# Sixteen instead of fourteen score blocks per quad get their maximum by a difference of keys, with a newly written order of TensorE's work

## The chip, the cores and the metric

The kernel runs on one core of a Trainium2 chip. A core has five engines with their own instruction queues: TensorE (PE, matrix products into PSUM), VectorE (DVE), ScalarE (ACT), GpSimd (POOL) and SyncE (SP, here only the issuer of DMAs). Each engine works through its queue in order and waits on semaphores. The metric is the device time of one execution in microseconds (us); lower is better. Times of an unchanged kernel vary a little: the three runs shown lie between 1987.35 and 1992.8 us.

## The reference

The input x is 4 batches of 2048 tokens with 256 features. After a layer norm, the result is x + attention(xn) + feed-forward(xn). The feed-forward part has ternary weights, an exact GELU and a second layer norm. The attention has 16 heads of 16 dimensions, with rotary embedding on 8 of them, and is causal:

```
scores = jnp.einsum('bhqd,bhkd->bhqk', q, k) * scale
causal = jnp.tril(jnp.ones((t, t), dtype=bool))
scores = jnp.where(causal[None, None], scores, -jnp.inf)
att = jax.nn.softmax(scores, axis=-1)
y = jnp.einsum('bhqk,bhkd->bhqd', att, v)
y = y.transpose(0, 2, 1, 3).reshape(b, t, c)
return y @ Wc
```

All arithmetic is float32 in the reference. The weights are large enough that the softmax needs each row's maximum subtracted.

## The kernel before, in words

The kernel has three stages. The weights are prepared, then a loop over 16 chunks of 512 tokens computes projections and the feed-forward part, and then comes attention, which is the only stage that the change touches. Attention works on 16 *quads*: four heads of one batch. For one quad, two streams run side by side.

**The stream for maxima** finds each query row's maximum before the exponentials may be taken. For every tile `t` of 128 queries, every head and every block `k` of 512 keys up to the causal limit, TensorE writes a block of scores, queries on the partitions, into one of three PSUM buffers `sm` (L1344), and VectorE reduces it to one number per row, `pm`. There are three kinds. A *plain* block is reduced by L1277. An *edge* block is cut by the causal limit, so it is 128 to 512 keys wide, and is reduced together with a mask (L1262). A *paired* block stands for two blocks of 512 keys, k = 0 and k = 1. Since max(a, b) = a + relu(b - a), TensorE computes b - a for two heads at once from a difference of keys `DK` (L1353) into a score buffer `st`, ScalarE takes its Relu into one of three buffers `excess` (L1194), and VectorE adds that to the block k = 0 in the same instruction that takes the maximum (L1273). So a pair of paired blocks costs one ScalarE instruction of 128 x 1024 and spares VectorE two plain blocks. L1262 and L1273 leave their number in an accumulator, which a second short instruction reads.

**The stream for outputs** computes scores again with keys on the partitions and the row's maximum folded in through two extra rows, in units of two heads: TensorE writes into one of two buffers `st` (L1365), ScalarE takes the exponential into one of eight buffers `prob` (L1201), GpSimd masks the diagonal ones (L1158), and TensorE multiplies by V for four heads (L1378, sums in `pv`), which ScalarE copies out at the end of each 512 queries (L1184). The differences share the two `st` buffers with the scores.

The stream for maxima runs ahead of the stream for outputs by `AHEAD` entries: while a quad's outputs are computed, its remaining entries and the first `AHEAD` entries of the next quad are done. Entries are the blocks and seven others: three transposes of the maxima (L1340, `("rows", n)`) and four output projections of an earlier quad (L1324), which `PROJECT_AT` places. `LEAD` says how many entries before its use a difference is issued in the prologue.

TensorE's order for one quad is a string, `TIMETABLE` (L804). Each letter is one step: `m` is the next entry for maxima, `x` the next difference, `s` one unit of scores (two heads; 80 per quad), `w` one weighted sum (four heads; 40 per quad, three steps behind the scores). ScalarE follows the same string, taking only its own steps; VectorE takes the entries in their order.

```
if c == "m":
    plan.append(("entry", e // NE, e % NE))
elif c == "x":
    plan.append(("excess", x // NX, x % NX))
elif c == "s":
    plan.append(("scores", 0, u))
else:
    plan.append(("sums", -1 if n < 0 else 0, n % PAIRS))
```

TensorE waits before a difference or a unit of scores until ScalarE has read the unit that was in that `st` buffer (`exp_done`), and before an entry until VectorE has read the `sm` buffer (`sm_read`). The last quad runs the same string without the next quad's steps, and with the last output projections at places counted from `AHEAD`.

Of the kernel before, what the change touches and what calls it, by code (L numbers as in the profile page):

```python
# [744 lines left out]
GROUP_OF = {c: n for n, cs in enumerate(GROUPS) for c in cs}  # L745
LATE = 4
LEAD = 7
PROJECT_AT = (78, 91, 107, 121)
EXCESSES = 3
ROWS_LOADED = 16 * 2 * G  # L750

# [1 line left out]
def maxima_sequence():  # L753


    sequence = []
    for n, cs in enumerate(GROUPS):
        blocks = []
        for t in range(SUB * cs[0], SUB * (cs[-1] + 1)):
            c = t // SUB  # L760
            for hp in range(G // 2):
                pair = c == 3 or c == 2 and (hp == 0 or t % 2 == 1)
                for k in range(c + 1):
                    if pair and k == 1:
                        continue
                    role = "edge" if k == c else "paired" if pair and k == 0 else "plain"
                    blocks += [(role, 2 * hp + g, t, k) for g in range(2)]
        last = blocks[-1]
        sequence += blocks[:LATE] + [("rows", (n - 1) % NG)] + blocks[LATE:-1] + [last + ("ends", n)]
    for s in reversed(range(SUB)):  # L770
        sequence.insert(PROJECT_AT[s], ("project", s))
    return sequence


SEQ = maxima_sequence()
NE = len(SEQ)
PAIRED = [e for e in range(NE) if SEQ[e][0] == "paired"]
# [9 lines left out]
WIDE = 2 * CH  # L787


AHEAD = 73  # L790
XAHEAD = sum(e < AHEAD + LEAD for e in EXCESS)
LAG = 3

# [3 lines left out]
def block_width(t, k):  # L797
# [4 lines left out]


TIMETABLE = (  # L804
    "mxsmwmsmmxmsmsmmwsmwxmsmwsmsmssmwmmxwsmmsmmsmmwmmxsmwmmsmxmmwsmmxwmm"
    "smsmmsmmswsmsmxmmswssmmmxwsmmwwsmmsmmsmmswsmmmswsmmsmwsmsmmwmmssmwsm"
    "msmmmsmwsmmmswxmmmswsmmxmswsmmsssmwmmsmsmmwwmmssmmwmsmmsmwmsmsmmwmss"
    "mmwmsmmswsmmmswmsmmsmswsmmmswmsmsmmwxmmswmmsmxmmwsmsmmwsmsmmxmmswsmm"
    "s"
)  # L810


def tokens():

    plan, e, x, u, n = [], AHEAD, XAHEAD, 0, -LAG
    for c in TIMETABLE:
# [9 lines left out]
        else:  # L826
            plan.append(("sums", -1 if n < 0 else 0, n % PAIRS))
            n += 1
    assert (e, x, u, n) == (NE + AHEAD, NX + XAHEAD, 2 * PAIRS, PAIRS - LAG)
    return plan  # L830
# [4 lines left out]

EXTRA = {LATE: NE, **{AHEAD - 2 * (2 * SUB - i) + 1: NE + 1 + i for i in range(2 * SUB)}}
LAST = [("entry", 0, EXTRA[x[2]]) if x[1] == 1 else x for x in FULL if x[1] < 1 or x[0] == "entry" and x[2] in EXTRA]
# [35 lines left out]
def attention(nc, io, w, scr):  # L873

    with ExitStack() as ctx:
# [337 lines left out]
        def _(dve):  # L1213
# [74 lines left out]
            dve.wait_ge(sm_read, SM)  # L1288
            for e in range(AHEAD):
                take(0, 0, e, False)  # L1290

            def body(quad, slot, last):
                for e in range(AHEAD, NE):
                    take(quad, slot, e, last)
                    if e == INVERT_LATE and quad:
                        invert(2 * quad - 1)
                if last:
                    split_rows(quad, slot, NE, NG - 1, NG)
                    invert(2 * quad)
                    for i in range(2 * SUB):  # L1300
                        add(quad, slot, NE + 1 + i, NCH - TC + i // SUB, i % SUB)
                    return
                for e in range(AHEAD):
                    if e == INVERT_EARLY:
                        invert(2 * quad)
                    take(quad + 1, (slot + 1) % SLOTS, e, quad + 1 == NQ - 1)
# [182 lines left out]
```

## Time and profile before

| | |
|---|---|
| median of 3 runs | 1990.69 us (1987.35 to 1992.8) |
| the profiled execution's own time | 1986.25 us |
| its span, first to last instruction | 1984.5 us |
| busy over the span: PE / DVE / ACT / POOL | 94% / 86% / 81% / 28% |
| matrix clock granted, mean | 0.971 of 2.4 GHz |

Attention begins at about 524 us of the span and is three quarters of it. The busy shares over the whole span mix it with the stages ahead of it, so for this change a window inside attention is read (650 to 1860 us, some 14 quads). Two cautions: durations of instructions that follow each other on one engine overlap, so what one more instruction costs is the distance between two starts and not the duration; and ends of matrix products are modelled, so a busy TensorE may have room.

### The profile page before, as it was taken

How to read it: one execution, taken by the hardware profiler on the slowest of the kernel's cores; microseconds unless marked ns; L12 is line 12 of the kernel's file. 1: busy time of each engine (PE TensorE's matmuls, PEld its weight loads, DVE VectorE, ACT ScalarE, POOL GpSimd, SP SyncE). 2: the span in 40 equal slices, each digit the busy share in tenths (PEclk: the TensorE clock that was granted, in tenths of full speed). 3: DMA queues.
4: the chain of work that ended last, by engine and by line, in shares of the span. 5: the costliest groups of instructions: out<-in, count | busy, mean ns of one | idle time of the engine just before them, and what ended most of it. 6: DMA issues, size and time to landing. Idle time of an engine off the chain costs nothing.

```text
span 1984.5 us, 42329 instructions
## 1 busy us (share of the span) xinstructions
PE 1863.5 (94%) x13873; PEld 697.3 (35%) x13873; DVE 1703.3 (86%) x4778; ACT 1613.8 (81%) x2110; POOL 558.1 (28%) x712
## 2 busy tenths in 40 slices
PE   6799999999689999999999999999999999999986
PEld 6455556555322222222232222223222222222223
DVE  5699999999888988989898898989899898989941
ACT  2466666676169999999999999999999999999992
POOL 0112211221413424142342414234241423424111
PEclk7899999999669999999999999999999999999998
DMA  4133332336531403032241414224141431414012
GB/s 170 36 92 100 100 90 85 94 100 137 98 68 28 66 19 65 18 61 45 53 69 37 71 33 83 45 53 69 37 74 30 83 53 45 69 37 77 18 40 76
DMA packets 161366, 130.36 MB, mean 66 GB/s; under 512 B 95360, under 2 KB 145792, under 8 KB 160808
## 3 DMA queue, kind: packets, MB, share of 16 engines
q1 hardware_dynamic: 161192, 128.21, 29.8%
q8 instruction: 88, 1.44, 0.3%
q14 instruction: 86, 0.70, 0.1%
HBM read 75.79 MB, written 42.99 MB: 60 GB/s over the span
## 4 chain that ended last, share of the span: by engine, by line
PE 45%; ACT 16%; issue 3%; DVE 3%; DMA 3%; SPq 2%; POOL 1%; ACTq 0%; DVEq 0%; POOLq 0%
PE pv L1378 19%; ACT prob L1201 13%; PE st L1365 11%; PE sm L1344 9%; ACT excess L1194 3%; PE sm L1324 3%; PE st L1353 3%; DMA scratch_i<-inverse 1%; DVE pm L1277 1%; DVE sm L1273 1%; DMA Yc<-Y 1%; PE sm L1340 1%; SPq L870 1%; DVE sm L1262 0%; DMA out<-Rt 0%
## 5 line engine op out<-in xcount | busy, mean ns | idle before, releaser
L1201 ACT ACTIVATE prob<-st 128x1024 f32<-128x1024 f32 (+3 forms) x1280 | 1078.7, 900 | 71.4 <-PE st L1365 59.1
L1378 PE MATMUL pv<-prob,V 128*32 128x512 f32 (+3 forms) x5120 | 593.9, 541 | 0.2
L1262 DVE CUSTOM_DVE_ANT_0 sm<-sm,mask 128x128 f32<-128x128 f32 (+3 forms) x1024 | 492.2, 511 | 64.2 <-PE sm L1344 51.9
L1344 PE MATMUL sm<-K,Q 48*128 48x512 f16 (+3 forms) x2112 | 524.7, 349 | 15.8 <-DVE pm L1277 4.3
L1365 PE MATMUL st<-Q,K 50*128 50x512 f16 (+3 forms) x2560 | 485.3, 353 | 28.2 <-ACT prob L1201 19.9
L1158 POOL TENSOR_SCALAR_AFFINE_SELECT prob<-prob 128x256 f32<-128x256 f32 x512 | 206.2, 409 | 944.1 <-ACT prob L1201 938.7
L1277 DVE TENSOR_REDUCE pm<-sm 128x1 f32<-128x512 f32 x640 | 416.9, 684 | 23.7 <-PE sm L1344 22.1
L1273 DVE CUSTOM_DVE_ANT_0 sm<-sm,excess 128x512 f32<-128x512 f32 x448 | 311.3, 716 | 33.0 <-PE sm L1344 25.9
L1344 PEld LDWEIGHTS sm<-K,Q 48*128 48x128 f16 x2112 | 167.5, 94 | 326.0 <-DVE pm L1277 159.0
L1365 PEld LDWEIGHTS st<-Q,K 50*128 50x128 f16 x2560 | 126.9, 93 | 427.7 <-ACT prob L1201 307.7
L1194 ACT ACTIVATE excess<-st 128x1024 f32<-128x1024 f32 x219 | 225.0, 1027 | 17.8 <-PE st L1353 11.1
L1378 PEld LDWEIGHTS pv<-prob,V 128*32 128x32 f32 x5120 | 104.1, 108 | 165.8 <-issue 113.1
L1262 DVE DVE_READ_ACCUMULATOR2_ANT pm<- 128x1 f32 x1024 | 145.4, 142 | 0.2
L639 ACT ACTIVATE g<-bank 128x512 f32<-128x512 f32 x128 | 76.7, 599 | 54.8 <-PE bank L708 54.8
L669 PE MATMUL bank<-wWP,gh 128*128 128x256 f16 x512 | 113.7, 273 | 0.0
L669 PE MATMUL bank<-wWP,gl 128*128 128x256 f16 x512 | 113.5, 272 | 0.0
L1353 PE MATMUL st<-DK,Q 48*128 48x512 f16 x448 | 94.3, 388 | 18.9 <-ACT prob L1201 14.9
L533 DVE SCALAR_TENSOR_TENSOR gl<-g,wlnw,gh 128x512 f16<-128x512 f32 x128 | 92.1, 761 | 6.7 <-ACT gh L642 6.7
L642 ACT ACTIVATE gh<-g,wlnw 128x512 f16<-128x512 f32 x128 | 93.6, 731 | 0.0
L475 POOL TENSOR_TENSOR frs<-fve,wmhalf 128x4 f32<-128x4 f32 x16 | 16.3, 1018 | 274.7 <-DVE fve L603 274.7
L1324 PE MATMUL sm<-Wc,Yc 128*128 128x256 f32 x256 | 72.6, 413 | 16.2 <-POOL Yc L1138 15.5
L644 ACT ACTIVATE g<-g 128x512 f32<-128x512 f32 x128 | 81.6, 637 | 0.0
(156 smaller groups left out, 1954.6 us busy)
## 6 DMA issues: line engine op xcount, KB each, us to landing
Q<-scratch_q SPq DMA_DIRECT2D x102, 128.0 KB, 4.4
K<-scratch_k SPq DMA_DIRECT2D x102, 128.0 KB, 7.3
x<-in_x SPq DMA_DIRECT2D x18, 512.0 KB, 4.4
scratch_v<-Vs SPq DMA_DIRECT2D x64, 128.0 KB, 2.0
scratch_r<-R SPq DMA_DIRECT2D x16, 512.0 KB, 3.2
V_raw<-scratch_v SPq DMA_DIRECT2D x16, 512.0 KB, 10.0
Rt<-scratch_r SPq DMA_DIRECT2D x16, 512.0 KB, 3.9
Yc<-Y SPq DMA_DIRECT2D x128, 64.0 KB
```

Of the source, the lines that this page charges most:

```text
L669: pe.matmul(bank[s][:, 0:C], lhsT=x[:, hc, s * P:(s + 1) * P], rhs=w["WP"][:, hc, :], start=hc + k == 0, stop=hc + k == HC)
L1158: pool.affine_select(out=x, in_=x, compare_op=ALU.is_ge, fill=0.0, base=0, pattern=[[0, 2], [1, P]], channel_multiplier=-1).then_inc(maske ...
L1194: act.activation(excess[((slot + ahead) % SLOTS * NX + k) % EXCESSES][:, :, :], st[number % ST][:, :, :], ACT.Relu)\
L1201: act.activation(prob[(slot * UNITS + k) % PT][:, :, 0:width], st[number % ST][:, :, 0:width], ACT.Exp)\
L1262: dve.tensor_tensor_reduce(x, x, mask[:, CH - width:], 1.0, -3e38, ALU.add, ALU.max, pm[:, row, t, k:k + 1]).then_inc(sm_read, 1)
L1273: dve.tensor_tensor_reduce(x, x, excess[(slot * NX + r) % EXCESSES][:, h % 2, :], 1.0, -3e38, ALU.add, ALU.max, pm[:, row, t, k:k + 1]).th ...
L1277: dve.tensor_reduce(out=pm[:, row, t, k:k + 1], in_=x, axis=AX.X, op=ALU.max).then_inc(sm_read, 1)
L1324: i = pe.matmul(dst[:, 0:C], lhsT=Yc[g // TC % 2][:, a, t:t + P], rhs=Wc[:, a, :], start=a == 0, stop=a == CC - 1)
L1344: pe.matmul(dst[:, 0:block_width(t, k)], lhsT=Q[slot][r, h // 2, t * P:(t + 1) * P], rhs=K[slot][r, h // 2, k * CH:k * CH + block_width(t, ...
L1353: i = pe.matmul(st[number % ST][:, g, :], lhsT=Q[slot][rows[g], h // 2, t * P:(t + 1) * P], rhs=DK[slot][rows[g], h // 2, :], start=True, ...
L1365: i = pe.matmul(st[number % ST][:, a, 0:width], lhsT=K[slot][r, u % 2, j * P:(j + 1) * P], rhs=Q[slot][r, u % 2, (c + 1) * CH - width:(c + ...
L1378: i = pe.matmul(pv[2 * DH * h:2 * DH * (h + 1), CH - width:CH], lhsT=V[quad % VSLOTS][:, j, h, :], rhs=prob[(slot * UNITS + 2 * n + h // 2 ...
```

## The change

In `maxima_sequence`, all blocks of the third group of 512 queries (c = 2) are now paired; before, one of four pairs of heads and tiles was plain. A quad then has 16 differences in place of 14, 32 paired blocks for 28, 32 plain ones for 40, and 135 entries for 139. `AHEAD` goes from 73 to 71; the prologue makes 7 differences for 5. `PROJECT_AT` and the whole `TIMETABLE` are new (273 letters before, 271 now); of the table two lines stand here.

```
-PROJECT_AT = (78, 91, 107, 121)
+PROJECT_AT = (74, 87, 103, 117)
...
-                pair = c == 3 or c == 2 and (hp == 0 or t % 2 == 1)
+                pair = c >= 2
...
-AHEAD = 73
+AHEAD = 71
...
-    "mxsmwmsmmxmsmsmmwsmwxmsmwsmsmssmwmmxwsmmsmmsmmwmmxsmwmmsmxmmwsmmxwmm"
...
+    "wmsmsmmsmsmmwwxsmmwsmxmmswsxmmsmwwsmxmmsmmmxmsmmsmwsmmmswmmsmwsmsmms"
...
```

VectorE, in the block for c = 2 of a middle quad, between two edge blocks of 384 keys and an addition of an output projection. L1262 and its kin are one line lower after the change. Before:

```order
L1262 ISA sm1,pm<-sm1,mask 128x384 [waits sm_ready,consts]
L1262 ISA sm2,pm<-sm2,mask 128x384 [waits sm_ready,consts]
L1277 TENSOR_REDUCE pm<-sm0 128x1 [waits sm_ready]
L1277 TENSOR_REDUCE pm<-sm1 128x1 [waits sm_ready]
L1277 TENSOR_REDUCE pm<-sm2 128x1 [waits sm_ready]
L1277 TENSOR_REDUCE pm<-sm0 128x1 [waits sm_ready]
L1262 ISA sm1,pm<-sm1,mask 128x384 [waits sm_ready,consts]
L1262 ISA sm2,pm<-sm2,mask 128x384 [waits sm_ready,consts]
L1246 TENSOR_TENSOR Rt0<-Rt0,sm0 128x256 [waits r_loaded,sm_ready]
```

The same place on VectorE after the change:

```order
L1261 ISA sm2,pm<-sm2,mask 128x384 [waits sm_ready,consts]
L1261 ISA sm0,pm<-sm0,mask 128x384 [waits sm_ready,consts]
L1272 ISA sm1,pm<-sm1,excess2 128x512 [waits sm_ready,consts,exp_done]
L1272 ISA sm2,pm<-sm2,excess2 128x512 [waits sm_ready,consts,exp_done]
L1261 ISA sm0,pm<-sm0,mask 128x384 [waits sm_ready,consts]
L1261 ISA sm1,pm<-sm1,mask 128x384 [waits sm_ready,consts]
L1245 TENSOR_TENSOR Rt0<-Rt0,sm2 128x256 [waits r_loaded,sm_ready]
```

The four plain blocks have become two paired ones, which wait for ScalarE's Relu (`exp_done`) besides TensorE.

TensorE, at the end of the string and the beginning of the next quad's. Q2,K2 belong to the quad whose outputs are computed, DK0,Q0 to the next one. Before:

```order
L1365 MATMUL st1<-Q2,K2 128x128 [waits exp_done]
L1344 MATMUL sm2<-K0,Q0 128x384 [waits sm_read]
L1344 MATMUL sm0<-K0,Q0 128x512 [waits sm_read]
L1365 MATMUL st0<-Q2,K2 128x128 [waits exp_done]
L1344 MATMUL sm1<-K0,Q0 128x512 [waits sm_read,qk_loaded1,v_placed]
L1353 MATMUL st1<-DK0,Q0 128x512 [waits exp_done,differed]
L1365 MATMUL st0<-Q0,K0 128x512 [waits exp_done,m_loaded]
L1344 MATMUL sm2<-K0,Q0 128x512 [waits sm_read]
L1378 MATMUL pv<-prob2,V1 32x384 [waits masked]
```

The same place on TensorE after the change:

```order
L1364 MATMUL st1<-Q2,K2 128x128 [waits exp_done]
L1343 MATMUL sm2<-K0,Q0 128x384 [waits sm_read]
L1364 MATMUL st0<-Q2,K2 128x128 [waits exp_done]
L1352 MATMUL st1<-DK0,Q0 128x512 [waits exp_done,differed]
L1343 MATMUL sm0<-K0,Q0 128x384 [waits sm_read]
L1352 MATMUL st0<-DK0,Q0 128x512 [waits exp_done,differed]
L1343 MATMUL sm1<-K0,Q0 128x512 [waits sm_read]
L1377 MATMUL pv<-prob2,V1 32x384 [waits masked,qk_loaded1,v_placed]
L1343 MATMUL sm2<-K0,Q0 128x512 [waits sm_read]
L1364 MATMUL st1<-Q0,K0 128x512 [waits exp_done,m_loaded]
```

Two differences now stand close together here, and the first one's own entries (into `sm1` and `sm2`) follow three and five letters of the string later; before, a difference stood at least 14 letters ahead of its entry. After the change six of the 16 stand 10 letters or fewer ahead of theirs (3, 3, 7, 7, 7 and 10).

## Rows read from the trace of the kernel before

**Rows 1.** The page's first part: span, busy us, share, instructions.

```profile
span 1984.5 us, 42329 instructions
PE 1863.5 (94%) x13873; PEld 697.3 (35%) x13873; DVE 1703.3 (86%) x4778; ACT 1613.8 (81%) x2110; POOL 558.1 (28%) x712
```

**Rows 2.** The page's 40 slices: matrix clock granted, in tenths.

```profile
PEclk7899999999669999999999999999999999999998
```

**Rows 3.** Stretches: us, busy (instructions) by engine, clock, DMA, GB/s.

```profile
650.00:1860.00 1210.00, 1165.55 (x9182) 335.97 (x9183) 1091.59 (x3337) 1139.24 (x1370) 405.32 (x558) 1.00 0.29 53
524.00:564.25 40.25, 31.99 (x85) 7.99 (x87) 37.75 (x125) 5.12 (x5) 16.96 (x10) 0.50 0.54 91
1866.00:1955.90 89.90, 83.54 (x630) 26.64 (x627) 43.95 (x124) 77.58 (x94) 15.61 (x34) 1.00 0.11 26
```

**Rows 4.** GpSimd's cast of DK, once per quad: one start, and the line's summary.

```profile
687.96 1.04 POOL L1128 CAST DK<-apart 128x1024 f16<-128x1024 f32 x1
...
L1128 POOL CAST DK<-apart x16: 1037/1037/1038, 538.6 to 1814.7; 128x1024 f16<-128x1024 f32 x16
```

**Rows 5.** Chain that ended last, 650 to 1860 us, shares by line.

```profile
by line: PE pv L1378 27.1%; ACT prob L1201 17.3%; PE st L1365 15.2%; PE sm L1344 13.2%; ACT excess L1194 4.6%; issue 4.4%; PE st L1353 3.9%; PE sm L1324 3.7%; DMA scratch_i<-inverse 2.0%; DVE pm L1277 1.5%; DVE sm L1273 1.3%; SPq L870 0.8%;
```

**Rows 6.** ACT in order of time: start, us, instructions (merged), idle before.

```profile
999.93 1.93 ACT L1201 ACTIVATE prob<-st 128x1024 f32<-128x1024 f32 x2
1001.74 1.04 ACT L1194 ACTIVATE excess<-st 128x1024 f32<-128x1024 f32 x1
...
1004.87 0.60 ACT L1184 ACTIVATE Y<-pv 128x512 f32<-128x512 f32 x1
1005.36 1.02 ACT L1194 ACTIVATE excess<-st 128x1024 f32<-128x1024 f32 x1
1006.27 1.35 ACT L1201 ACTIVATE prob<-st 128x512 f32<-128x512 f32 x3
```

**Rows 7.** DVE in order of time.

```profile
1003.82 0.73 DVE L1273 CUSTOM_DVE_ANT_0 sm<-sm,excess 128x512 f32<-128x512 f32 x1
1004.47 0.14 DVE L1273 DVE_READ_ACCUMULATOR2_ANT pm<- 128x1 f32 x1
1004.47 0.73 DVE L1262 CUSTOM_DVE_ANT_0 sm<-sm,mask 128x512 f32<-128x512 f32 x1
...
1009.55 0.70 DVE L1273 CUSTOM_DVE_ANT_0 sm<-sm,excess 128x512 f32<-128x512 f32 x1
1010.17 1.28 DVE L1277 TENSOR_REDUCE pm<-sm 128x1 f32<-128x512 f32 x2
1011.37 0.27 DVE L1228 TENSOR_SCALAR mh<-sm 16x128 f16<-16x128 f32 x1
```

**Rows 8.** ACT's groups, 650 to 1860 us: busy us, mean ns, idle before, releaser.

```profile
L1201 ACT ACTIVATE prob<-st 128x1024 f32<-128x1024 f32 (+3 forms) x1118 | 942.4, 900 | 55.2 <-PE st L1365 44.3 <-issue 0.7
L1194 ACT ACTIVATE excess<-st 128x1024 f32<-128x1024 f32 x196 | 201.3, 1027 | 15.6 <-PE st L1353 9.8 <-DVE pm L1277 0.3
```

**Rows 9.** DVE's three large groups, the same window and columns.

```profile
L1262 DVE CUSTOM_DVE_ANT_0 sm<-sm,mask 128x256 f32<-128x256 f32 (+3 forms) x894 | 430.2, 511 | 56.2 <-PE sm L1344 44.9 <-issue 0.4
L1277 DVE TENSOR_REDUCE pm<-sm 128x1 f32<-128x512 f32 x560 | 364.9, 684 | 19.5 <-PE sm L1344 18.0
L1273 DVE CUSTOM_DVE_ANT_0 sm<-sm,excess 128x512 f32<-128x512 f32 x390 | 271.0, 716 | 28.4 <-PE sm L1344 22.0 <-ACT prob L1201 1.1 <-ACT excess L1194 0.5
```

**Rows 10.** PE in order of time: a sum between scores and entries.

```profile
1297.55 1.06 PE L1378 MATMUL pv<-prob,V 128*32 128x512 f32 x8
1298.55 0.39 PE L1365 MATMUL st<-Q,K 50*128 50x512 f16 x2
1298.78 0.38 PE L1344 MATMUL sm<-K,Q 48*128 48x512 f16 x1
```

**Rows 11.** ACT at 1295 to 1303 us, beside rows 10.

```profile
1294.98 5.99 ACT L1201 ACTIVATE prob<-st 128x1024 f32<-128x1024 f32 x6
1301.39 1.94 ACT L1201 ACTIVATE prob<-st 128x1024 f32<-128x1024 f32 x2 [0.41 <-PE st L1365]
```

More of the change, by code:

```diff
@@ L804 @@
 TIMETABLE = (
-    "mxsmwmsmmxmsmsmmwsmwxmsmwsmsmssmwmmxwsmmsmmsmmwmmxsmwmmsmxmmwsmmxwmm"
[L806 to L809, printed above, removed]
+    "wmsmsmmsmsmmwwxsmmwsmxmmswsxmmsmwwsmxmmsmmmxmsmmsmwsmmmswmmsmswmsmms"
+    "mmxsmmwsmmxmswsmsmmxsmwxmmwwsmmsmmsmmswsmmmswsmmswsmmmswsmmsmmswsmmm"
+    "smmsmwsmmmswsmmmxwsmmxmswsmmsxmswmmsmsmmwwmmssmmwmmsmsmwsmmmswsmmmsw"
+    "mmsmswmmsmswsmmmswsmmswsmmmswmsmsmmwxmmswsmmmswsmmxmmswsmmsmsmsxmxm"
 )
```

## The prediction

> **What bounds the kernel now.** I read first the busy line and the clock slices. Over the span TensorE, VectorE and ScalarE are all above 80% [rows 1], and the clock is full through attention apart from its start [rows 2], so neither a single engine nor the clock explains the time. Then the window inside attention: of 1210 us TensorE's rows cover 96%, ScalarE's 94% and VectorE's 90% [rows 3]. GpSimd's cast, which comes once per quad, starts at 687.96 us in the third quad and at 1814.7 us in the sixteenth [rows 4]: 13 periods in 1126.7 us, 86.67 us per quad. The window so holds 13.96 quads.
>
> Busy shares overstate the load, since durations overlap. Two exponentials take 1.93 us together, where one takes 1.02, so a unit starts 0.91 us after the one before it; a copy of `pv` is followed after 0.49 us [rows 6]. With 56 full units, 14 differences, 4 copies and 24 narrower units (8 each of 384, 256 and 128 columns per head; I estimate 0.71, 0.49 and 0.28 us, their durations less the same overlap of 0.11) ScalarE needs 51.0 + 12.7 + 2.0 + 11.8 = 77.5 us per quad. VectorE: a plain block 0.60 us (two of them from 1010.17 to 1011.37), a paired one 0.65, as from 1003.82 to 1004.47, or 0.62 at the least, as from 1009.55 to 1010.17 [rows 7]. With the edges (64 at 0.45, an estimate from their mean of 511 ns [rows 9], less the same kind of overlap) and 3.3 us of small work, estimated, it needs about 74.4 us. So ScalarE has 9.2 us and VectorE 12.3 us per quad in which they could do more. Whom they wait for: ScalarE 54 us in the window, all but for 0.3 for TensorE [rows 8]; VectorE 85 us for TensorE, 1.6 for ScalarE [rows 9]. And TensorE waits for both through the buffers. The time is lost in the coupling of three nearly full engines in fixed order: a weighted sum holds TensorE for 1.00 us before the next scores can start [rows 10], longer than a ScalarE unit, and ScalarE runs dry after it. Beside these rows six units take 5.99 us, 0.99 apart where 0.91 is possible, and then 0.41 us pass empty [rows 11]. The chain goes 63% through TensorE, 22% through ScalarE and 3% through VectorE's two named lines [rows 5].
>
> **The change, part by part.**
>
> *Two more differences on ScalarE*, per quad: 2 x 0.91 = +1.82 us of demand, 77.5 to 79.3 [rows 6].
>
> *VectorE:* 8 plain blocks go, 4 paired come: -8 x 0.60 + 4 x 0.65 = -2.2 us, 74.4 to 72.2 [rows 7].
>
> *TensorE:* four entries fewer, two pairs of difference products more. I price these by the chain, which has only what counted: L1344 holds 13.2% of 86.67 = 11.4 us over 132 blocks, 0.087 each; L1353 3.4 us over 14, 0.24 each [rows 5]. -4 x 0.087 + 2 x 0.24 = +0.13 us. GpSimd and the DMA queues get nothing new: DK is made once per quad whatever the number of differences, and the loads are the same.
>
> *What of the 1.82 lies beside other work.* First estimate, by the chain: ScalarE's lines are 21.9% of it, 19.0 us of 77.5 us of its work, so an added us is on the path for 0.245 of itself: +0.45. VectorE: 2.8%, 2.4 us of 74.4: -0.07. TensorE +0.13. Sum +0.5 us per quad. This assumes the old order. Second estimate, by the new order: I cut each string into ten stretches of eight scores units, and add for each what ScalarE and VectorE need by the prices above. The larger of the two, summed, is 80.1 us before (the second stretch for example 10.5 to 9.6, the fifth 7.3 to 6.0, the last 6.6 to 7.6, there VectorE's) and 80.3 after (10.5 to 9.3, 7.3 to 6.3, 7.5 to 7.1). That is +0.2: in four of ten stretches VectorE had been the larger, and there the added units fill time that ScalarE could not use. I take +0.2, since it sees the new order, with +0.5 inside. The bounds are far apart: all of the added work on the path, +1.82; all of VectorE's relief, -2.2. Between them the order decides, and no row of before shows it: which units find TensorE in a sum is new at every place.
>
> *Moved work.* `PROJECT_AT` and the transposes keep their places within four letters (the first projection at letter 7 for 11, the last transpose at 138 for 140), and the products are the same: 0. The sums still stand three behind.
>
> *Prologue.* 71 entries for 73 at VectorE's pace, which is busy for 37.75 of 40.25 us there while ScalarE is for 5.12 [rows 3]: -5 x 0.60 + 3 x 0.65 = -1.05 us; two more pairs of products at half clock give part back. I take -0.6, from -1.05 to +0.5. *Last quad:* 9 differences and 80 scores units as before, two entries fewer on VectorE, which is busy for 43.95 of 89.9 us: 0 [rows 3]. Cover lost here would cost 0.6 us at most.
>
> *Sum.* 15 periods x 0.2 = +3.0, less 0.6: +2.4 us on a profiled execution of 1986.25 (span 1984.5 and 1.75 around it). The median of the runs is 4.4 us above that execution; the same step on the median gives 1993.1.
>
> **The rivals.**
>
> *B, ScalarE becomes the bound (slower).* If the gaps before ScalarE's units are set by TensorE's sums and not by VectorE, they do not shrink when ScalarE has more to do, and the differences come on top. For it: ScalarE is the fuller of the two by rows and is 22% of the chain against 3%. Against it: the gaps are 9.2 us per quad, and the new order may place the differences in them. Between half and all of 1.82 us, 1.37 x 15 = +20.5, less 0.6: 2010.6; at full price 2017. It decides from where ScalarE's 9.2 us per quad do not fall below 8.3. The Trainium skill's page "Perfetto Trace Analysis" (Identifying the Most-Contended Engine) says to find the engine with the highest occupancy among VectorE, ScalarE and GpSimd and to optimize that first; here that is ScalarE, 94% against 90%, and the change moves work onto it. By that rule this rival is what happens. The trace agrees with the occupancies, and the chain with the sign, but not with its size.
>
> *C, VectorE's relief and the order get through (faster).* For it: VectorE waited for TensorE in 85 us of the window, and each such wait, once TensorE had come late, was handed back through three `sm` buffers; 2.2 us less work lets it catch up sooner. Three entries in a row before a unit of scores ("mmms") stand 10 times in the string for 6, places at which TensorE can refill all three `sm` buffers before it goes on. A difference's buffer has been read 11 letters or more before it is wanted again, for 6 before. If 1.0 us per quad goes, between 0.5 and 2.2: -15 less 0.6: 1975. Against it: the chain hardly touches VectorE.
>
> *D, VectorE waits for ScalarE (slower).* Six differences stand close ahead of their entries. At the end of the string the difference has at most one unit in front of it on ScalarE, so its Relu ends about 2 x 0.91 + 0.2 us after the product was issued, and TensorE, which needs `exp_done` of that same unit before it can issue the next difference or scores, brings the entry 1.2 to 1.6 us after. A wait of 0.2 to 0.8 us at six places: 1.2 to 4.8 us per quad on VectorE. Behind the waiting block stand the other two `sm` buffers, and then TensorE's next entry, and the scores behind that. VectorE has 12.3 us free, so I charge a fifth to a quarter, at most 1.0 us: +15, 2005. Before, such waits were 1.6 us in the whole window.
>
> ScalarE's price per element also speaks on the choice of engine. A Relu unit of 1024 columns takes 0.91 us and spares two plain blocks of 512, 1.20 us, at 2 x 0.05 more for the paired ones. The Trainium skill's page "ScalarE: Activation LUTs" (Rules for kernel authors) says to put relu and max on VectorE and not on ScalarE. By the rule moving them is a loss; on these float32 blocks out of PSUM the trace has ScalarE the faster one per column, 0.89 ns against 1.17, so I do not follow it beyond rival B.
>
> **How the numbers follow.** This kernel's measurement tells about 0.3%, 6 us, from no change. My forecast, the loads nearly cancel, has 0.36, with an own range of -0.4 to +0.6 us per quad, 1984 to 2000; of it 0.04 are faster by more than 6 us, 0.05 slower, 0.27 the same. C has 0.34, of which 0.01 is within 6 us. B has 0.24, D 0.06, together 0.28 slower and 0.02 the same. Faster 0.37, same 0.30, slower 0.33. The range takes in C to a little beyond its middle and B to its middle: 1973 to 2011.
>
> **What would show it.** Counts per quad: 16 Relus, 32 paired and 32 plain blocks. The period by GpSimd's cast: 86.9 us if I am right, 85.7 under C, 88.0 under B. ScalarE's idle in a window of 14 quads: 71 us before [rows 8]; in my case it falls to about 50, in B it stays near 65, in C it falls to 40 or below. VectorE's waits on exponentials or Relus: under 10 us in the window if D is wrong, 17 to 67 if it is right. VectorE's share falls from 90% to about 87%, and under C its waits for TensorE fall as well. I am wrong if the period moves by more than 0.6 us either way, and wrong in kind if the difference lies in the prologue or the last quad.

## The result: 0.28% faster, and the profile after

| | before | after |
|---|---|---|
| median (14 runs each) | 1991.54 us (1985.04 to 1995.04) | 1985.78 us (1981.33 to 1988.33) |
| profiled execution, its span | 1986.25, 1984.5 us | 1983.96, 1982.0 us |

The ratio is 0.9972, 95% interval 0.9962 to 0.9982: a small gain, clear of noise, at the edge of what I had called no change, and on the other side of the forecast of 1993.

The page's first two parts for the changed kernel; they answer to [rows 1, 2].

```profile
span 1982.0 us, 42489 instructions
PE 1851.7 (93%) x13873; PEld 695.8 (35%) x13873; DVE 1669.6 (84%) x4778; ACT 1637.0 (83%) x2142; POOL 556.0 (28%) x712
...
PEclk8899999999769999999999999999999999999998
```

ScalarE has 23 us more of busy rows, VectorE 34 us less. The stretch 650 to 1860 us, for [rows 3]:

```profile
650.00:1860.00 1210.00, 1157.20 (x9196) 335.77 (x9198) 1064.00 (x3343) 1160.73 (x1400) 404.87 (x560) 1.00 0.29 53
```

ScalarE's share went from 94% to 96%, VectorE's from 90% to 88%. GpSimd's cast of DK, one start per quad, before (two more than in [rows 4]) and after:

```profile
1034.28 1.04 POOL L1128 CAST DK<-apart 128x1024 f16<-128x1024 f32 x1
1121.28 1.04 POOL L1128 CAST DK<-apart 128x1024 f16<-128x1024 f32 x1
```

```profile
1035.48 1.04 POOL L1127 CAST DK<-apart 128x1024 f16<-128x1024 f32 x1
1121.82 1.04 POOL L1127 CAST DK<-apart 128x1024 f16<-128x1024 f32 x1
...
1812.68 1.04 POOL L1127 CAST DK<-apart 128x1024 f16<-128x1024 f32 x1
```

From 1121 us on eight periods take 86.68 us each before (to 1814.7) and 86.36 after. ScalarE's groups and its idle time after, for [rows 8]:

```profile
L1200 ACT ACTIVATE prob<-st 128x1024 f32<-128x1024 f32 (+3 forms) x1120 | 942.6, 902 | 22.3 <-PE st L1364 13.1
L1193 ACT ACTIVATE excess<-st 128x1024 f32<-128x1024 f32 x224 | 229.0, 1029 | 26.2 <-PE st L1352 10.6 <-PE st L1364 5.5 <-DVE pm L1261 4.8
```

The recorded idle before them fell from 71 to 49 us in 14 quads. VectorE's, for [rows 9]:

```profile
L1261 DVE CUSTOM_DVE_ANT_0 sm<-sm,mask 128x256 f32<-128x256 f32 (+3 forms) x895 | 431.7, 511 | 74.5 <-PE sm L1343 68.0 <-issue 0.4
L1272 DVE CUSTOM_DVE_ANT_0 sm<-sm,excess 128x512 f32<-128x512 f32 x448 | 307.0, 718 | 50.5 <-PE sm L1343 40.4 <-ACT prob L1200 7.0
L1276 DVE TENSOR_REDUCE pm<-sm 128x1 f32<-128x512 f32 x448 | 290.7, 682 | 11.7 <-PE sm L1343 10.2
```

VectorE waits more for TensorE, 119 us for 85. Its lighter load turned into waiting. The chain, 650 to 1860 us, for [rows 5]:

```profile
by line: PE pv L1377 28.3%; PE st L1364 16.0%; ACT prob L1200 13.2%; PE sm L1343 10.7%; issue 7.7%; ACT excess L1193 6.4%; PE st L1352 3.2%; PE sm L1323 3.0%; ACT Y L1183 1.7%; SPq L1012 1.7%; DVE sm L1272 1.5%; DMA Yc<-Y 1.4%; DVE pm L1276
```

By lines the chain hardly moved: TensorE 61% for 63%, ScalarE 21% for 22%. ScalarE's first units of the quads, read in order of time, split the span. The unchanged kernels ran twice with a profile, so there are two of each (us):

| | start | quads 1 to 4 | quads 5 to 15 | last quad to the end | span |
|---|---|---|---|---|---|
| before | 564.3 | 348.0 | 953.7 | 118.5 | 1984.5 |
| before, again | 564.3 | 352.6 | 954.1 | 118.6 | 1989.5 |
| after | 564.1 | 350.7 | 950.2 | 117.0 | 1982.0 |
| after, again | 565.5 | 353.0 | 950.3 | 117.2 | 1986.0 |

The gain is in the settled quads, -3.5 and -3.8 us over eleven, and in the last one, -1.5 and -1.4. Start and first four quads give some back, +2.5 and +1.6. The share of the last quad hangs on the cut: before, a quad's first unit is a Relu, after the change it is the first scores. Cut at the first scores in both, the last quad gives -0.7 and -0.5, start and first four quads +1.6 and +0.7, and the settled quads the same as above. The profiles give -2.5 and -3.5 in all, the medians -5.8: some 2 to 3 us of the timed difference no profile shows.

### The profile page after: what moved, and what is told of

Read it like the earlier page. It is cut to its first block, busy times and chain, and to the rows that moved or that the text cites. A ratio compares the mean times of both kernels' runs of the same rounds, so it can differ in the third digit from the quotient of the medians.

```text
span 1982.0 us, 42489 instructions
## 1 busy us (share of the span) xinstructions
PE 1851.7 (93%) x13873; PEld 695.8 (35%) x13873; DVE 1669.6 (84%) x4778; ACT 1637.0 (83%) x2142; POOL 556.0 (28%) x712
## 4 chain that ended last, share of the span: by engine, by line
PE 43%; ACT 16%; issue 6%; DVE 4%; SPq 2%; DMA 2%; POOL 1%; ACTq 0%; DVEq 0%; POOLq 0%
PE pv L1377 19%; PE st L1364 11%; ACT prob L1200 10%; PE sm L1343 7%; ACT excess L1193 4%; PE sm L1323 2%; PE st L1352 2%; ACT Y L1183 1%; SPq L1012 1%; DVE sm L1272 1%; DMA Yc<-Y 1%; DVE sm L1261 1%; DVE pm L1276 1%; SPq L1009 1%; PE sm L1339 0%
## 5 line engine op out<-in xcount | busy, mean ns | idle before, releaser
L1343 PE MATMUL sm<-K,Q 48*128 48x512 f16 (+3 forms) x2048 | 476.3, 348 | 14.4 <-DVE pm L1276 6.7
L1272 DVE CUSTOM_DVE_ANT_0 sm<-sm,excess 128x512 f32<-128x512 f32 x512 | 350.9, 718 | 60.4 <-PE sm L1343 49.0
L1276 DVE TENSOR_REDUCE pm<-sm 128x1 f32<-128x512 f32 x512 | 332.2, 683 | 16.1 <-PE sm L1343 14.4
L1193 ACT ACTIVATE excess<-st 128x1024 f32<-128x1024 f32 x249 | 254.7, 1029 | 29.2 <-PE st L1352 12.1
L1343 PEld LDWEIGHTS sm<-K,Q 48*128 48x128 f16 x2048 | 155.4, 95 | 249.7 <-DVE pm L1261 87.0
L1352 PE MATMUL st<-DK,Q 48*128 48x512 f16 x512 | 108.0, 390 | 20.2 <-ACT prob L1200 11.9
```

What stands on the lines that cost most here:

```text
L1193: act.activation(excess[((slot + ahead) % SLOTS * NX + k) % EXCESSES][:, :, :], st[number % ST][:, :, :], ACT.Relu)\
L1272: dve.tensor_tensor_reduce(x, x, excess[(slot * NX + r) % EXCESSES][:, h % 2, :], 1.0, -3e38, ALU.add, ALU.max, pm[:, row, t, k:k + 1]).th ...
L1276: dve.tensor_reduce(out=pm[:, row, t, k:k + 1], in_=x, axis=AX.X, op=ALU.max).then_inc(sm_read, 1)
L1343: pe.matmul(dst[:, 0:block_width(t, k)], lhsT=Q[slot][r, h // 2, t * P:(t + 1) * P], rhs=K[slot][r, h // 2, k * CH:k * CH + block_width(t, ...
L1352: i = pe.matmul(st[number % ST][:, g, :], lhsT=Q[slot][rows[g], h // 2, t * P:(t + 1) * P], rhs=DK[slot][rows[g], h // 2, :], start=True, ...
```

## The experiments

**Two more differences in the old order.** The sixteen-difference sequence, and the string of before with the letters of the four vanished entries taken out and two x put in (first and last piece):

```
-    "mxsmwmsmmxmsmsmmwsmwxmsmwsmsmssmwmmxwsmm...
+    "mxswsmmxmsmsmmwsmwxmsmwsmsmssmwmmxwsmm...
...
-    ...wmsmsmmwxmmswmmsmxmmwsmsmmwsmsmmxmmswsmms"
+    ...wmsmsmmwxswmmsmxmmwsmsmxmwsmsmmxmmswsmms"
```

> Sixteen differences with the order of before: the old string without the letters of the four entries that vanish, and with the two new differences put 5 letters after the one of the pair before (L-string places 155 and 257). Theory 1, the new order brings the gain and the two differences cost: slower than before by 0.3 to 1% (ScalarE's added 1.82 us per quad is on the path for 0.25 to 0.7 of itself), 1998 to 2010 us. Theory 2, VectorE's relief of 2.2 us brings the gain and the order little: 1983 to 1988 us, as the changed kernel.

Measured 1.0187 (1.0155 to 1.0219), 2028.9 us: slower than either theory gave. The next run has the fourteen-difference sequence with the string of after, two x out and four m in.

> Fourteen differences with the order of after: the new string without the two added differences and with the four plain entries put back, one at each of four places. Theory 1 (the order brings the gain): ratio 0.990 to 0.996, below the changed kernel, since ScalarE has 1.82 us per quad less to do. Theory 2 (VectorE's relief does): 1.000 to 1.006, VectorE 2.2 us per quad more and late somewhere.

Measured 1.0075 (1.0047 to 1.0103). That also is slower, so Theory 1 in its plain form falls too: the new order is not a better one whatever it holds. For where, I cut the eleventh quad's time by ScalarE's starts of scores units 0, 8, 16, ... (us; the sum is the period):

| | 1 | 2 | 3 | 4 | 5 | 6 | 7 | 8 | 9 | 10 | sum |
|---|---|---|---|---|---|---|---|---|---|---|---|
| before | 7.96 | 12.48 | 6.85 | 9.10 | 8.07 | 7.99 | 8.17 | 8.28 | 8.77 | 8.86 | 86.52 |
| old order, 16 | 7.96 | 12.48 | 6.84 | 9.09 | 8.07 | 9.04 | 8.17 | 8.28 | 8.77 | 10.18 | 88.88 |
| after | 9.07 | 9.98 | 8.90 | 8.97 | 7.54 | 8.89 | 8.01 | 7.82 | 8.85 | 8.39 | 86.41 |
| new order, 14 | 10.06 | 9.98 | 8.90 | 8.97 | 7.54 | 8.49 | 8.01 | 7.82 | 9.38 | 8.24 | 87.40 |

Stretches that were not edited keep their time to 0.01 us. (The second profile of before has 7.86 in the sixth and 86.39 in all.) A difference added to the old order costs 1.05 us in the sixth stretch, more than its 0.91 on ScalarE, and 1.32 in the tenth; the two plain entries less in the first and the two in the ninth give nothing back. Taking one out of the new order gives 0.40 and 0.15 back, and the entries put in cost 0.99 and 0.53.

**The same with the letters elsewhere.** Both strings again, edited at other places; first a piece of the old order with sixteen, then one of the new with fourteen:

```
-    ...swxmmmsxwsmmxmsw...
+    ...swxmmmswsmxmxmsw...
...
-    "wmsmmsmmmsmsmmwwxsmm...
+    "wmmsmsmmsmmsmmwwxsmm...
```

> Sixteen differences in the order of before, with the two new letters x at other places than in old_order_16 (158 and 252 of the old string for 155 and 257). If two more differences in the old order cost a full ScalarE unit each, as the stretches of old_order_16 say (+1.05 and +1.32 us per quad, where nothing else was added), the ratio is 1.014 to 1.020 again. If it was the place, under 1.010.

> Fourteen differences in the order of after, with two other letters x left out and the four m at other places. If the new order only suits its own contents: 1.004 to 1.012 again. If it was the places: near 0.996 or below, since ScalarE has 1.8 us per quad less to do than in the changed kernel.

Measured 1.0130 (1.0097 to 1.0163) and 1.0062 (1.0042 to 1.0082). The old order's price falls by a quarter (sixth and tenth stretch 8.95 and 9.65): between the two ratios that I had expected, so the place counts for some of it, but most of the loss stays. The new order's stays as it was. Two sets of places each support that the parts alone lose. They don't exclude a fourteen-difference string near the new one that is good.

**The unchanged kernels again.**

> The kernel before, unchanged, for a second profile and for what the comparison tells of no change: ratio within 0.2% of 1. If the order of before is sensitive to small shifts of timing, its periods per quad differ again by up to 1 us among each other, at other quads than in the first profile; if these are a fixed pattern, the same quads are long again.

> The changed kernel, unchanged, for a second profile: ratio 0.996 to 0.998. If the new order settles to one period, the quads from the eighth on take 86.34 us each again, to 0.1 us.

Measured 1.0006 (0.9988 to 1.0024) and 0.9976 (0.9959 to 0.9992). The pattern of before is fixed in part: the fifth quad takes 86.72 us and the sixth 86.98 in both profiles, but the seventh 86.92 and 86.51, and the thirteenth 86.64 and 87.74. Over the eleven settled quads that comes to 0.3 us. After the change seven of the quads 7 to 15 take 86.34 or 86.35, the other two 86.38 and 86.41 or 86.42, in both profiles. What differs most between two runs sits in the first quads: the fourth took 85.74 and 89.75 us before, 85.94 and 88.17 after. Before, again, in the slow one of these:

```profile
832.50:842.00 9.50, 9.49 (x56) 1.77 (x56) 6.27 (x18) 6.18 (x9) 1.95 (x5) 0.50 0.18 30
```

The clock is at 0.50, that is 1.2 GHz, TensorE is busy all the time and ScalarE for two thirds of it. In the first profile the same place has 1.00:

```profile
820.00:840.00 20.00, 19.07 (x165) 5.76 (x157) 18.75 (x60) 18.97 (x27) 6.13 (x16) 1.00 0.16 36
```

**Whose work counts.** In each kernel a part of one engine's work is left out, so that the maxima or the sums come out incomplete, while the other engines' work in attention stays the same. Relus on half the columns:

```
-act.activation(excess[...][:, :, :], st[number % ST][:, :, :], ACT.Relu)
+act.activation(excess[...][:, :, 0:CH // 2], st[number % ST][:, :, 0:CH // 2], ACT.Relu)
```

> The kernel before, with each Relu taken on 512 of the 1024 columns; the other half of the excess buffers is zero, so half of the paired maxima lack their key difference. TensorE and VectorE do the same work; ScalarE has 14 x 0.42 = 5.9 us per quad less (estimate from 1024 columns at 0.91 us and a copy of 512 at 0.49). By the chain (an added us of ScalarE on the path for 0.25 of itself) -1.5 us per quad, 1967 us. If ScalarE is the bound (rival B): -4 us per quad or more, under 1930. If VectorE is (rival C): less than 0.3 per quad, over 1984.

> The changed kernel with each Relu on 512 of the 1024 columns (the same part left out): ScalarE has 16 x 0.42 = 6.7 us per quad less. If the change moved the bound towards ScalarE, this gains clearly more than the same cut in the kernel before: -2.5 to -4 us per quad, 1925 to 1948. If it stayed a matter of coupling: -1.7 us per quad, 1960.

Plain maxima over half the keys:

```
-dve.tensor_reduce(out=pm[:, row, t, k:k + 1], in_=x, axis=AX.X, op=ALU.max)
+dve.tensor_reduce(out=pm[:, row, t, k:k + 1], in_=x[:, 0:CH // 2], axis=AX.X, op=ALU.max)
```

> The kernel before, with each plain block's maximum over 256 of its 512 keys, so plain maxima are over half the keys: VectorE has 40 x 0.27 = 10.8 us per quad less, nothing else changes. By the chain (VectorE's own lines 3%): -0.4 to -1 us per quad, 1976 to 1984. If VectorE's lateness sets the gaps (rival C, that of which the change would take 2.2 us): -3 us per quad or more, under 1946.

> The changed kernel with plain maxima over 256 of 512 keys: VectorE has 32 x 0.27 = 8.6 us per quad less. If the relief of VectorE brought the gain and there is more of it to have, -2 us per quad or more, under 1956. If VectorE's work no longer counts: -0.5 us per quad at most, 1978 or more.

Narrower sums on TensorE (24 of 40 per quad):

```
+wide = min(width, 384) if j else width
-i = pe.matmul(pv[..., CH - width:CH], ..., rhs=prob[...][:, h % 2, 0:width], ...
+i = pe.matmul(pv[..., CH - wide:CH], ..., rhs=prob[...][:, h % 2, width - wide:width], ...
```

> The kernel before with 384 of 512 columns in the 24 weighted sums per quad that are full and not the first of their 512 queries; their first 128 queries lack these terms. TensorE has 24 x 0.21 = 5.0 us per quad less (1.00 us against 0.79 for the narrower sum in the chain). If TensorE's sums set the gaps (chain: TensorE 63%, on the path for 0.75 of its work): -3.8 us per quad, 1934 us. If it is no more on the path than ScalarE (0.11 by the cut of the Relus): -0.6 per quad, 1981.

> The changed kernel with the same narrower sums: -5.0 us per quad of TensorE's work. If the new order took weight off TensorE (ScalarE is now on the path for 0.26 of its work and was for 0.11), it gains less than before did from this cut: -2 to -3 us per quad, 1940 to 1955. If the order changed nothing for TensorE: -3.8 per quad, 1929.

| cut, us of work per quad | ratio in before | weight | ratio in after | weight |
|---|---|---|---|---|
| ScalarE, 5.9 and 6.7 | 0.9951 (0.9915 to 0.9987) | 0.11 | 0.9838 (0.9810 to 0.9867) | 0.27 |
| VectorE, 10.8 and 8.6 | 0.9981 (0.9959 to 1.0003) | 0.02 | 0.9986 (0.9962 to 1.0011) | 0 |
| TensorE, 5.0 | 0.9801 (0.9776 to 0.9826) | 0.53 | 0.9804 (0.9777 to 0.9832) | 0.45 |

The weight is the time gained per us of work taken away, over 15 quads; for after it is counted from 0.9973. The work taken away is an estimate from distances between starts. VectorE can lose about an eighth of its work and nothing clear of noise moves in the timed runs of either kernel; the settled quads of the profiles give 0.2 and 0.1 us each for it. Rival C's account, VectorE's relief, falls. ScalarE counts more than twice as much after the change; the settled quads of the profiles say so too, with 0.06 before and 0.22 after. TensorE counts somewhat less (the two intervals overlap, so that is only indicated).

ScalarE's group in the old order with half Relus shows where most of its cut went:

```profile
L1201 ACT ACTIVATE prob<-st 128x1024 f32<-128x1024 f32 (+3 forms) x1126 | 948.6, 896 | 126.7 <-PE st L1367 121.0 <-issue 0.2
L1194 ACT ACTIVATE excess<-st 128x512 f32<-128x512 f32 x198 | 117.9, 596 | 16.1 <-PE st L1355 10.8
```

The Relus are 83 us shorter in the window and the exponentials wait 77 us longer for TensorE (121.0 for 44.3).

**The last quad.** The last quad's plan comes from the other order, the rest stays:

```
+OTHER = tokens(LAST_TABLE)
-LAST = [... for x in FULL if x[1] < 1 or ...]
+LAST = [... for x in OTHER if x[1] < 1 or ...]
```

> The kernel before in its first fifteen quads, the last one in the order of after (that with fourteen differences, as in new_order_14): only the order inside the last quad differs. In the profiles the stretch from the last quad's first ScalarE unit to the end took 118.5 us before, 117.0 after and 117.3 with that order. If the last quad is a part of the gain by itself: 117.3 here too, -1.3 us, ratio 0.9993. If it only inherits how the fifteenth quad leaves the engines: 118.5, ratio 1.

> The changed kernel with the last quad in the order of before (that of old_order_16). If the last quad is a part of the gain by itself: its stretch grows from 117.0 to 118.5 us, and the ratio from 0.9973 to about 0.998. If not: 117.0.

Measured 1.0007 (0.9997 to 1.0018) and 0.9995 (0.9982 to 1.0009). In the profiles the last stretch is 117.6 and 118.7 us. The two orders begin with different units, so only the last quad and the one ahead of it together tell. In after, the old last quad costs 1.6 us (118.7 for 117.0, and 86.21 for 86.34 ahead of it); into before the new one brings 0.3 (-1.0, and 87.30 for 86.60 ahead of it). The ratio for after points the same way (0.9995 against 0.9972 to 0.9976, intervals touching or overlapping). That for before doesn't: its interval lies above the 0.9993 that a gain by itself would give. By these runs the last quad's order counts with the new order ahead of it and hardly with the old one. A part of the 1.6 us can be misfit, since the old order here is that made over for sixteen differences.

**The close differences (rival D) and the place of a single letter.** First all six close differences earlier:

```
-    "wmsmsmmsmsmmwwxsmmwsmxmmsw...
+    "wmsmsmmsmsmmxwwsmmxwsmmmsw...
...
-    ...wsmmxmmswsmmsmsmsxmxm"
+    ...wsxmmmmswsmmsmxsmxsmm"
```

> The changed kernel with the six differences that stand close to their entries 1 to 3 letters earlier in the string. Theory D (VectorE waits for them and that costs): up to 0.5 us per quad faster, ratio 0.993 to 0.996. Against it (the profile after has 7 us of such waits in 14 quads, and VectorE's work halved at plain blocks moved nothing): 0.997 to 1.003, by what the shifted units do to ScalarE's gaps.

Measured 1.0151 (1.0133 to 1.0168): 35 us slower than the changed kernel, outside both expectations. VectorE's waits for ScalarE hardly changed by it, 6.8 us in the window for 7.0, so this run says nothing on what these waits cost. Then three of them, only past the two letters ahead:

```
-    "mmxsmmwsmmxmswsmsmmxsmwx...
+    "xmmsmmwsxmmmswsmsxmmsmwx...
```

> The changed kernel with three differences (letters 70, 78 and 87) issued ahead of the two entries or the letters before them; ScalarE's gaps there are 0.58, 0.26 and 0.39 us per quad. If the two products ahead make the gap, which on TensorE take 0.2 to 0.4 us and may wait for VectorE: -0.5 us per quad, ratio 0.993 to 0.995, a version that beats both. If the wait only moves to the next unit: 0.997 as the changed kernel.

Measured 1.0027 (1.0015 to 1.0040): 11 us slower than the changed kernel, not faster. The eleventh quad has 87.33 us for 86.41, and its third stretch alone 9.77 for 8.90. In the run before, with only the first of the three moved in that stretch (letter 70 to 68), it is 9.77 too. So that one letter, moved by two places, costs 0.87 us per quad. TensorE in order of time at this place, after:

```profile
1453.37 0.34 PE L1364 MATMUL st<-Q,K 50*128 50x384 f16 x2
1453.64 1.13 PE L1323 MATMUL sm<-Wc,Yc 128*128 128x256 f32 x4
1454.70 0.39 PE L1343 MATMUL sm<-K,Q 48*128 48x512 f16 x1
1454.71 0.60 PE L1352 MATMUL st<-DK,Q 48*128 48x512 f16 x2
```

The same in the experiment:

```profile
1457.95 0.34 PE L1364 MATMUL st<-Q,K 50*128 50x384 f16 x2
1458.96 0.39 PE L1352 MATMUL st<-DK,Q 48*128 48x512 f16 x2 [0.67 <-ACT prob L1200]
1459.28 1.13 PE L1323 MATMUL sm<-Wc,Yc 128*128 128x256 f32 x4
1460.35 0.39 PE L1343 MATMUL sm<-K,Q 48*128 48x512 f16 x1
1460.35 0.33 PE L1364 MATMUL st<-Q,K 50*128 50x384 f16 x1
```

ScalarE there, in the changed kernel:

```profile
1455.41 1.02 ACT L1193 ACTIVATE excess<-st 128x1024 f32<-128x1024 f32 x1 [0.47 <-PE st L1364]
1456.33 1.29 ACT L1200 ACTIVATE prob<-st 128x768 f32<-128x768 f32 x2
```

And in the experiment:

```profile
1459.45 1.02 ACT L1193 ACTIVATE excess<-st 128x1024 f32<-128x1024 f32 x1
1460.94 0.81 ACT L1200 ACTIVATE prob<-st 128x768 f32<-128x768 f32 x1 [0.47 <-PE st L1364]
1462.52 0.60 ACT L1200 ACTIVATE prob<-st 128x512 f32<-128x512 f32 x1 [0.77 <-PE st L1364]
```

The difference needs an `st` buffer that ScalarE still reads. In the changed kernel TensorE does an output projection of 1.06 us in that time. Issued directly, the difference stops TensorE for 0.67 us, and the projection comes afterwards, where it delays the next scores: ScalarE stands idle twice, 0.47 and 0.77 us, where the changed kernel has 0.47 once. The other two that were moved cost next to nothing (the third stretch is 9.77 with or without the second of them, the fourth 9.03 for 8.97), so it is the place that counts, not the moving.

## Why the prediction was wrong

*The step that failed* is the second estimate under "What of the 1.82 lies beside other work", the stretches of eight scores units, and so the term of +0.2 us per quad. Measured are -0.3 us in the settled quads (86.68 to 86.36). The estimate took what a quad needs beyond its larger loads, 86.67 - 80.1 = 6.6 us, as a constant, without a reason. It is not: by the same working, redone with my estimated prices, the old order with sixteen differences comes to 80.2 us at either set of places, +0.1, and was measured at +2.36 and +1.73. At one place the traces show what the loads can't see: whether a product that must wait for a buffer has work ahead of it in the string that fills the wait. Two letters' distance moved 0.87 us per quad there, four times the whole term, with the loads of the stretch unchanged. That the new order's gain over the old is made of such places was not shown one by one.

*The sizes.* Two added differences cost as much as rival B says and more, where the order isn't made for them: +2.36 us per quad for 1.82 of work (86.52 to 88.88), 1.73 with the other places. The new order takes that back and 0.1 to 0.3 more. Next to nothing comes from VectorE's 2.2 us: at the weight 0.02 of its cut they are 0.05 us per quad. Rival C had the right sign with the wrong engine: its 1.0 us per quad from VectorE's relief is refuted, and an order that fits is what is left of it.

*The chain as a measure of weight.* It gave ScalarE 0.245 and VectorE 0.03; for TensorE an expectation above has 0.75, while 63% of 86.67 us over its 83.5 us of busy rows per quad would be 0.65. The cuts gave 0.11, 0.02 and 0.53 in before. The ranking was right, but ScalarE's was 2.2 times and TensorE's 1.2 to 1.4 times too high. ScalarE's weight after the change, 0.27, is near what I had taken for before; that is chance, for the chain gives ScalarE no more after the change than before it.

*Rival D* is wrong: VectorE's waits for ScalarE are 7 us in the window, below the 10 I had set, and VectorE's own work has next to no weight. *The prologue*, -0.6: the start of the first quad's units moved by -0.2 and +1.2, but that holds the stages ahead too. From GpSimd's first cast of DK to the first unit it is 25.7 us before and 26.0 after, in both profiles of each; to the first exponential it is 28.0 and 26.0. So the term is small with either sign, by where one cuts. *The last quad*, priced at 0, gave -0.5 to -1.5 by where one cuts. Even so it wouldn't have turned the sign with the period at +0.2. *The range* held the time, and so did the narrower 1984 to 2000 of my own case; it was the sign that failed.

*The signs I named* came in oddly: ScalarE's recorded idle fell from 71 to 49 us, as set for my case, while the period came out at 86.4, between my 86.9 and C's 85.7. The period moved by less than the 0.6 us that I had named as the sign of being wrong: that bound was too wide to see the change's effect.

*What stays open.* The 2 to 3 us between the profiles' gain and the medians'; what brings the half clock in the first quads, and what ends it; and how much is owed to the order and how much to the sixteen differences, for the runs don't have the two apart: each order did best with its own contents, as far as tried.

## What to carry to other kernels

In this kernel, whose in-order engines are all near 90% busy, neither shares nor summed loads priced a move of some per cent from one engine to another. Where a trace shows the price, it was set at a single place, by whether an instruction that will block has independent work ahead of it; look for such places first. Take an engine's weight from a run with a part of its work cut away, and when part of a fixed order's contents changes, count on the loss of the whole fit (0.9 to 1.9% in the four runs here) unless the order is made anew.

## What the runs showed of the hardware

I had not expected the clock to fall once attention is running. Of the four profiles of unchanged kernels three have stretches at half clock in the first four quads, and TensorE shows no idle time of more than 0.55 us in the 14 us ahead of any of them; the longest is the one above. That quad took 4.0 us more than its twin, which is most of what separates the two spans of before (1984.5 and 1989.5). The first profile of before, on which the prediction rests, had none from 576 to 1958 us.

The new order meets such falls more often. Each order has three profiles whose first four quads are unedited: the two of the unchanged kernel and the one with another last quad. In them the clock, once full, falls again 0, 1 and 1 times with the old order and 3, 4 and 4 times with the new one. But with the new order it is full earlier, at 571 to 573 us for 576, 576 and 587, so that the time at half clock within the four quads is 11.9, 22.1 and 28.3 us with the old order and 20.9, 27.8 and 27.7 with the new one. What that costs or saves on average, three profiles each don't tell.
